# Giving the float32r operands of a fused attention and FFN kernel new start addresses in SBUF

## The reference, cut to what matters

```python
x = x + xattn(layernorm(x), ctx_768)   # q = ln(x)@Wq+bq ; k, v from ctx (77 rows) ; softmax over 77 ; @Wo+bo
x = x + ffn(layernorm(x))
def ffn(x):
    P = x @ U1                 # 512 -> 128
    H = gelu(P @ V1 + b1)      # 128 -> 2048
    Q = H @ U2                 # 2048 -> 128
    return Q @ V2 + b2         # 128 -> 512
```

## Time and profile before

| | |
|---|---|
| median of 3 runs | 558.01 us (557.27 to 558.16) |
| the profiled execution | 557.01 us, of which the profile's span is 555.2 us |
| PE busy | 545.4 us (98% of the span) |
| PEld busy | 463.6 us (84%) |
| DVE busy | 474.4 us (85%) |
| POOL busy | 374.1 us (67%) |
| ACT busy | 308.8 us (56%) |
| mean granted TensorE clock | 0.999 |

### The profile page before, as it was taken

The page is one execution under the profiler, slowest core; times in us unless marked ns, Lnnn a source line. Parts: engine busy times, 40 slices in busy tenths (PEclk is TensorE's granted clock), DMA queues, the critical chain, the costliest instruction groups (busy, mean ns, idle before and its releaser), DMA issues.

```text
span 555.2 us, 12052 instructions
## 1 busy us (share of the span) xinstructions
PE 545.4 (98%) x4824; PEld 463.6 (84%) x4824; DVE 474.4 (85%) x693; ACT 308.8 (56%) x518; POOL 374.1 (67%) x296
## 2 busy tenths in 40 slices
PE   8999999999999999999999999999999999999996
PEld 8998889888988898889877777888888888888885
DVE  5789989888988898889899568989889797978694
ACT  3655454545554555454455546757575757666563
POOL 3788776778777877786679356747474656565581
PEclk9999999999999999999999999999999999999999
DMA  8432352221223123243422130031121212101012
GB/s 322 171 85 73 124 223 92 97 105 53 94 96 116 43 94 97 91 148 125 137 68 78 64 113 2 19 105 47 63 89 59 76 73 81 57 19 58 20 57 94
DMA packets 25263, 50.36 MB, mean 91 GB/s; under 512 B 2936, under 2 KB 3064, under 8 KB 24824
## 3 DMA queue, kind: packets, MB, share of 16 engines
q1 hardware_dynamic: 24920, 49.07, 25.4%
q10 hardware_dynamic: 288, 0.52, 0.3%
HBM read 32.49 MB, written 16.78 MB: 89 GB/s over the span
## 4 chain that ended last, share of the span: by engine, by line
PE 85%; DVE 7%; POOL 3%; ACT 2%; issue 1%; DMA 1%; SPq 0%; DVEq 0%; POOLq 0%; ACTq 0%
PE bank L1037 50%; PE ps_s L1037 15%; PE bank L1115 6%; PE ps_s L1089 5%; PE bank L1131 5%; PE bank L1162 2%; PE bank L1058 2%; DVE once L860 1%; DMA fw<-in_Wk 1%; DVE ssum L828 1%; POOL wqo_r L409 1%; POOL ss L420 1%; DVE wqo_r L865 1%; DVE hs_r L883 1%; POOL ss L428 1%
## 5 line engine op out<-in xcount | busy, mean ns | idle before, releaser
L511 POOL TENSOR_TENSOR hs_r<-ss,hs_r 128x512 fp32r<-128x512 f32 x63 | 88.0, 1397 | 91.5 <-ACT hs_r L733 91.5
L646 ACT ACTIVATE ss<-ps_s,once 128x512 f32<-128x512 f32 x128 | 88.0, 689 | 64.9 <-PE ps_s L1037 61.4
L1037 PE MATMUL ps_s<-p1t_r,v_r 128*128 128x512 f32 x384 | 111.1, 398 | 0.0
L1037 PE MATMUL bank<-hs_r,u_r 128*128 128x512 f32 x381 | 107.2, 390 | 0.0
L1037 PE MATMUL bank<-zt_r,wqo_r 128*128 128x256 f32 x768 | 97.8, 283 | 0.2 <-ACT qt L542 0.2
L420 POOL TENSOR_TENSOR ss<-ss,smax 128x1232 f32<-128x1232 f32 x32 | 74.8, 2338 | 33.1 <-DVE smax L823 33.1
L1037 PE MATMUL bank<-wqo_r,ot_r 128*128 128x512 f32 x384 | 95.5, 398 | 0.0
L1037 PEld LDWEIGHTS bank<-zt_r,wqo_r 128*128 128x128 f32 x768 | 91.8, 188 | 1.5 <-issue 0.4
L1037 PEld LDWEIGHTS bank<-hs_r,u_r 128*128 128x128 f32 x381 | 71.4, 188 | 15.7 <-DVE hs_r L883 0.2
L1037 PEld LDWEIGHTS bank<-wqo_r,ot_r 128*128 128x128 f32 x384 | 69.8, 188 | 13.4 <-DVE ot_r L836 0.2
L1037 PEld LDWEIGHTS ps_s<-p1t_r,v_r 128*128 128x128 f32 x384 | 69.8, 188 | 13.4 <-issue 0.4
(11 more groups left out here) (97 smaller groups left out, 816.9 us busy)
## 6 DMA issues: line engine op xcount, KB each, us to landing
xs<-in_x SPq DMA_DIRECT2D x64, 256.0 KB, 3.3
y_between<-xs SPq DMA_DIRECT2D x32, 256.0 KB, 2.0
fw<-y_between SPq DMA_DIRECT2D x4, 1024.0 KB, 5.5
xs<-y_between SPq DMA_DIRECT2D x4, 1024.0 KB, 5.5
out<-fw SPq DMA_DIRECT2D x16, 256.0 KB, 2.0
out<-xs SPq DMA_DIRECT2D x16, 256.0 KB, 2.0
ss<-in_wq SPq DMA_DIRECT2D x2, 512.0 KB, 7.2
xs<-in_Wo SPq DMA_DIRECT2D x1, 1024.0 KB, 9.2
```

Of the source, the lines that this page charges most:

```text
L511: pool.tensor_tensor(hs[:, c % 4, 1, :], hg[:, c % 4, :], hs[:, c % 4, 0, :].bitcast(F32), ALU.subtract)\
L646: act.activation(hg[:, c % 4, :], ps_s[:, c % 4, :], ACT.Gelu_apprx_tanh, bias=b1_c[:, c:c + 1]).then_inc(h_gelu, 1)
L1037: mm = pe.matmul(ps, lhs(a), rhs(c), start=first and i == 0, stop=last and i == len(PASSES) - 1)
```

## The change

Only the declarations of the SBUF tensors change. No instruction is added, removed or moved on any engine or queue, and no wait. Three things are done:

1. The small tensors (`ident`, the statistics, the maxima and sums) are declared first, and the filler `lead` shrinks from 480 to 32 floats. Together they end at 18432 = 9 x 2048, and they keep their distances from a multiple of 2048.
2. The float32r tensors are declared in another order and two are widened by 8 floats or so, so that starts shift by 32 bytes (`ASIDE` = 8 floats).
3. The filler `rest` goes.

The tensors from `xs` to `bias_row` keep their addresses to the byte. Start of each operand, in bytes over a multiple of 2048, worked out from the declarations:

| product | weights before, after | moving before, after |
|---|---|---|
| q projection | `wq_r` 0, 0 | `zt` 32, 32 |
| output projection | `ot` 0, 0 | `wo_r` 0, 32 |
| U1 | `u1_r` 0, 0 | `z2t` 0, 32 |
| V1 | `v1_r` 0, 0 | `p1t` 0, 32 |
| U2 | `u2_r` 0, 0 | `hs` 0, 32 |
| V2 | `q2t` 0, 0 | `v2_r` 0, 0 |

Single operands inside these lie at multiples of 512 bytes (weights) or 1024 or 2048 bytes (moving) from there.

```diff
-LEAD = 480
+LEAD = 32
 ASIDE = 8
...
-        sb("lead", [P, LEAD])
-        wqo_r = sb("wqo_r", [P, 2 * 2 * KD * D], F32R)
-        wq_r = wqo_r[:, 0:2 * KD * D].rearrange("p (h k n) -> p h k n", h=2, k=KD)
-        wo_r = wqo_r[:, 2 * KD * D:].rearrange("p (h k n) -> p h k n", h=2, k=KD)
-        v1_t = sb("v1_r", [P, 2 * FF], F32R)
-        zt_t = sb("zt_r", [P, 2 * KD * TA + ASIDE], F32R)
-        zt = zt_t[:, ASIDE:].rearrange("p (h k t) -> p h k t", h=2, k=KD)
-        sb("rest", [P, 512 - ASIDE])
-        p1t = sb("p1t_r", [P, 2, 2, TB], F32R)
-        q2t = sb("q2t_r", [P, 2, TB], F32R)
-        ot = sb("ot_r", [P, 2, G, TA], F32R)
-        u2_r = sb("u2_r", [P, 2, NFF, R], F32R)
-        hs = sb("hs_r", [P, 4, 2, TB], F32R)
-
-        z2t = wqo_r[:, 0:2 * KD * TB].rearrange("p (h k t) -> p h k t", h=2, k=KD)
-        u1_r = zt_t[:, 0:2 * KD * R].rearrange("p (h k n) -> p h k n", h=2, k=KD)
-        v2_r = zt_t[:, 2 * KD * R:2 * KD * R + 2 * D].rearrange("p (h n) -> p h n", h=2)
...
         ident = sb("ident", [P, P])
         mhalf = sb("mhalf", [P, UB])
         eps_c = sb("eps_c", [P, UB])
...
         rsum = sb("rsum", [P, 4, H])
-
+        sb("lead", [P, LEAD])
+
+        wqo_r = sb("wqo_r", [P, 2 * 2 * KD * D + ASIDE], F32R)
+        wq_r = wqo_r[:, 0:2 * KD * D].rearrange("p (h k n) -> p h k n", h=2, k=KD)
+        wo_r = wqo_r[:, 2 * KD * D + ASIDE:].rearrange("p (h k n) -> p h k n", h=2, k=KD)
+        z2t = wqo_r[:, ASIDE:2 * KD * TB + ASIDE].rearrange("p (h k t) -> p h k t", h=2, k=KD)
+        p1t = sb("p1t_r", [P, 2, 2, TB], F32R)
+        hs = sb("hs_r", [P, 4, 2, TB], F32R)
+        zt_t = sb("zt_r", [P, 2 * KD * TA + D - ASIDE], F32R)
+        zt = zt_t[:, 0:2 * KD * TA].rearrange("p (h k t) -> p h k t", h=2, k=KD)
+        u1_v2 = zt_t[:, D - ASIDE:]
+        u1_r = u1_v2[:, 0:2 * KD * R].rearrange("p (h k n) -> p h k n", h=2, k=KD)
+        v2_r = u1_v2[:, 2 * KD * R:2 * KD * R + 2 * D].rearrange("p (h n) -> p h n", h=2)
+
+        v1_t = sb("v1_r", [P, 2 * FF], F32R)
+        q2t = sb("q2t_r", [P, 2, TB], F32R)
+        ot = sb("ot_r", [P, 2, G, TA], F32R)
+        u2_r = sb("u2_r", [P, 2, NFF, R], F32R)
```

More of the change, by code:

```diff
@@ L88, in sem @@
             return stack.enter_context(nc.semaphore(name))
+        ident = sb("ident", [P, P])
+        mhalf = sb("mhalf", [P, UB])
+        eps_c = sb("eps_c", [P, UB])
+        stall = sb("stall", [P, 1])
+        stats = sb("stats", [P, 4, 6])
+        stats_b, mv_b, var_b, rstd_b = (sb(n, [P, UB, w]) for n, w in (
+            ("stats_b", 6), ("mv_b", 2), ("var_b", 1), ("rstd_b", 1)))
+        mv = sb("mv", [P, 4, 2])
+        var_e = sb("var_e", [P, 4])
+        rstd = sb("rstd", [P, 4])
+        z_shift = sb("z_shift", [P, 4])
+        smax = sb("smax", [P, 4, H])
+        ssum = sb("ssum", [P, 4, H])
+        rsum = sb("rsum", [P, 4, H])
         sb("lead", [P, LEAD])
-        wqo_r = sb("wqo_r", [P, 2 * 2 * KD * D], F32R)
+        wqo_r = sb("wqo_r", [P, 2 * 2 * KD * D + ASIDE], F32R)
         wq_r = wqo_r[:, 0:2 * KD * D].rearrange("p (h k n) -> p h k n", h=2, k=KD)
-        wo_r = wqo_r[:, 2 * KD * D:].rearrange("p (h k n) -> p h k n", h=2, k=KD)
+        wo_r = wqo_r[:, 2 * KD * D + ASIDE:].rearrange("p (h k n) -> p h k n", h=2, k=KD)
[7 more added lines that the diff above has]
+        v2_r = u1_v2[:, 2 * KD * R:2 * KD * R + 2 * D].rearrange("p (h n) -> p h n", h=2)
         v1_t = sb("v1_r", [P, 2 * FF], F32R)
         v1_r = v1_t[:, :].rearrange("p (h n) -> p h n", h=2)
-        zt_t = sb("zt_r", [P, 2 * KD * TA + ASIDE], F32R)
-        zt = zt_t[:, ASIDE:].rearrange("p (h k t) -> p h k t", h=2, k=KD)
-        sb("rest", [P, 512 - ASIDE])
-        p1t = sb("p1t_r", [P, 2, 2, TB], F32R)
         q2t = sb("q2t_r", [P, 2, TB], F32R)
@@ L149, in xattn_ffn @@
         bq_c, bk_c, b1_c = bias_c[:, 0:G], bias_c[:, G:2 * G], bias_c[:, 2 * G:]
[L150 to L163, removed]
         bank = [stack.enter_context(nc.psum_tensor(f"bank{i}", [P, 512], F32)) for i in range(4, 8)]
```

## The result

The changed kernel takes 563.28 us (median of 6 runs, 563.02 to 564.03), the kernel before 558.0 us (6 runs). The ratio is 1.0098, 95% interval 1.0087 to 1.0109: about **1% slower**, 5.3 us. The forecast was 554.7 us, 0.6% faster.

A forecast was written before the change was run, and what follows sets the result against it. PE (TensorE) was taken as the bound. A gain of 2.9 ns on each of 1155 matmuls, 3.3 us, with all else at 0, took the median from 558.0 to 554.7 us; range 547 to 560.5.

The forecast's parts named there:

- What bounds the kernel: Whole kernel: PE busy 98% of the span and 85% of the chain; a shorter matmul counts fully in both long stretches.
- The excess of 13.3 and 10.4 ns: Float32r matmuls: time beyond a column per cycle, 13.3 ns at 512 columns, 10.4 at 256, where an address could act.
- Order, small tensors and distances of kilobytes at 0: SBUF declarations: new order, small tensors first, and operand distances changed by many kilobytes were taken to be worth 0.
- q and V2 unchanged: q projection (768 matmuls) and V2 (96): moving operand stays where it was relative to 2048, so 0 was taken.
- The price of the 32 bytes: Output projection, U1, V1, U2: moving operands 32 bytes over, forecast gain 3.3 us, bounded by 15.4 gain and 6.9 loss.
- the nearest row: the q projection: q, already at 32, has excess 10.4 against 13.3 ns; so each touched matmul gains 2.9 ns, 3.3 us in all.
- The 109.6 ns between the two forms: Pace difference between 512-column and 256-column matmuls in the rows, taken to confirm a column per cycle (106.7 ns for 256).
- the 24 matmuls of `zt_r` between 282 and 342 us: Stage changeover: counted as q and subtracted from 174 matmuls; half the rest, 70, were taken as touched on the path.
- 1155: Touched 512-column matmuls counted on the path: 305 in attention, 780 in FFN, 70 in the changeover between them.
- the offset puts TensorE in its slower pace: Rival for V1, U2, U1, output projection: 232 to 233 ns becomes settled; fully 6.9 us, 565 us; chance 0.14.
- Worth nothing: Rival: the 32-byte offset under the moving operands changes nothing; 557 to 559 us, near 558.0; chance 0.25.
- the evidence taken from weights at 0, 512, 1024 and 1536: FFN run of 15: weights at these starts over 2048 share one pace, so such distances to the moving operand do nothing.

## Why the prediction was wrong, step by step

**What bounds the kernel**: right. PE stays at 98% and 85% of the chain, and a change in the pace of TensorE went into the time in full (5.4 us of busy time in the four products, 5.3 us of median).

**The excess of 13.3 and 10.4 ns is where an address acts**: right, and the only place where anything moved.

**Order, small tensors and distances of kilobytes at 0**: right, 558.07 us with them alone. **q and V2 unchanged**: right, 97.8 and 24.0 us.

**The price of the 32 bytes**: here it failed. The step was "the nearest row: the q projection", with the sentence "if the 32 bytes are what separates the two figures, each touched matmul gains 2.9 ns". The condition was true: q at distance 0 costs 120.0 ns and at 32 it costs 117.1. The consequence was false: a 512-column matmul at 32 does not gain 2.9 ns but loses 6.7 in the run of fifteen, and 3.1 (V1) to 6.2 (U1) in the mean of its group. The same shift has opposite signs for the two lengths. The text named what it left out, that q streams half as long beside the same load, and then used q for the sign as well as for the size. A row of another shape does not give the sign of a cost.

Two readings of the rows were off and did not decide. The 109.6 ns between the two forms, read as a column per cycle, compared a product at distance 0 with one at 32; with both at 0 the difference is 226.7 - 120.0 = 106.7 ns, 256 cycles to the digit. And the 24 matmuls of `zt_r` between 282 and 342 us are U1 and not q (5.75 us / 24 is 240 ns each), so that U1 has six blocks and not seven between 342 and 547 us. The two slips nearly cancel: 1155 becomes some 1160.

**The rival that the time went to** was "the offset puts TensorE in its slower pace", given 0.14. Its figure was right: 232 to 233 ns became the settled pace, 233.3. That it is the same state is not shown, since the gaps behind a transpose follow no cycle of three. Its full price of 6.9 us was too high, and 5.4 us is what the groups show. One reason is in the rows: behind the transposes the matmuls were slow already and did not get slower (0.70 and 1.39 us before, 0.69 and 1.40 after), and the sum had counted them all at 6 ns. The argument held against it, that q at 32 shows no such pace, was the false step again.

**"Worth nothing"**, given 0.25, does not hold for float32r streams: moving one operand against the other by 32 bytes changed the pace by 6.7 ns at the same clock. The Trainium skill (SBUF — State Buffer, on the two separate sides; TensorE: Matmul & The Clock Gate, Part 2) gives TensorE two independent read ports, from which the prediction had drawn that start addresses change nothing; these traces do not agree with that conclusion. A shift by whole lines is not free either: at 16 bytes the 15 in a row already take 3.47 us. The prediction had its lines of 16 bytes from the Trainium skill (Advanced Engine Details and Errata, SBUF Cachelines). And the evidence taken from weights at 0, 512, 1024 and 1536 was sound but said less than it was used for: if the pattern repeats every 256 bytes, these four are one and the same distance.

**What stays open** is the mechanism beneath. Shown: the distance between the two operands changes the settled pace of float32r matmuls; 0 and 256 are alike; what is best for the 512-column products is among the worst for q. At 16 bytes what runs before q matters as much as the distance (113.3 or 118.6 ns). Not shown: that the 256 columns are the reason why q differs, since no run changed them alone; and whether the distance that counts is to a matmul's own weights or to those of the next one, loaded beside it, since within a product both start alike. That the two reads meet in the same part of SBUF is a reading that fits, and no run here shows it.

## What to carry to other kernels

For float32r products that follow one another without a gap, the starts of the weights and of the moving operand are a setting of their own, worth some 1% when TensorE is the bound, as it is here. Set it for each shape of matmul: here the products of 512 columns want a distance of 0 or 256 bytes, and the one of 256 columns wants 16 or 32 bytes more. Test one product at a time and read the pace from a run of matmuls in the chain, since what suits one shape costs another.

## What the runs showed that was not expected

- The excess is exact: 32 cycles at distance 0 for both lengths (226.7 - 213.3 and 120.0 - 106.7 ns), 48 cycles at 32 for 512 columns.
- The kernel with shorter weight loads (135 instead of 187 ns) streams more slowly, 230 instead of 226.7 ns.
- What a product takes depends a little on what ran before it. U1 at distance 0 takes 23.6 us behind a U2 at 32 and 23.3 behind one at 0. The output projection at 0 takes 96.2 us with every operand at 0 and 95.6 with every operand at 32; why is open.
